# Attention scores in two PSUM banks in place of four, written one slot ahead by two ordered pairs of row groups

## The reference, cut to what matters

```python
# second (_L2_xattn_ref)
scores = jnp.einsum('bhqd,bhkd->bhqk', qh, kh) / jnp.sqrt(dh)
scores = jnp.where(merged == 1, NEG_INF, scores)
attn = jax.nn.softmax(scores, axis=-1)
out = jnp.einsum('bhqk,bhkd->bhqd', attn, vh)
# last (_L3_xattn_ref)
scores = jnp.einsum('bhqd,bhkd->bhqk', q, k) / jnp.sqrt(jnp.float32(dh))
scores = jnp.where(scores == 0, NEG_INF, scores)
attn = jax.nn.softmax(scores, axis=-1)
```

## Time and profile before

| | |
|---|---|
| median of 3 runs | 1098.03 us (1096.59 to 1098.26) |
| the profiled execution's own time | 1100.99 us |
| its span, first to last instruction | 1099.2 us |
| PE busy | 911.5 us, 83% |
| DVE busy | 556.6 us, 51% |
| ACT busy | 444.9 us, 40% |
| POOL busy | 392.7 us, 36% |
| mean granted clock of TensorE | 0.890 |

### The profile page before, as it was taken

The page is one execution under the profiler, slowest core; times in us unless marked ns, Lnnn a source line. Parts: engine busy times, 40 slices in busy tenths (PEclk is TensorE's granted clock), DMA queues, the critical chain, the costliest instruction groups (busy, mean ns, idle before and its releaser), DMA issues. The chain is left out here.

```text
span 1099.2 us, 18929 instructions
## 1 busy us (share of the span) xinstructions
PE 911.5 (83%) x5718; PEld 623.4 (57%) x5719; DVE 556.6 (51%) x1282; ACT 444.9 (40%) x874; POOL 392.7 (36%) x726
## 2 busy tenths in 40 slices
PE   6688887888699999935888889997999997888773
PEld 4466655776566666723555556653666674555441
DVE  4688865674722222227988735220211235767854
ACT  4355555552132222214555542221222225656634
POOL 5566642364400000036766512110000035766630
PEclk9799999996599999975878999998999996988965
DMA  5599510011211111127310030002111121110002
GB/s 182 156 365 385 183 48 1 20 49 39 101 57 58 61 58 61 53 75 275 136 32 18 2 130 30 23 30 72 38 48 48 39 43 23 16 16 11 2 1 77
DMA packets 74397, 84.17 MB, mean 77 GB/s; under 512 B 8299, under 2 KB 66643, under 8 KB 74323
## 3 DMA queue, kind: packets, MB, share of 16 engines
q1 hardware_dynamic: 68179, 70.65, 19.1%
q0 software_dynamic: 6144, 12.59, 4.2%
HBM read 45.73 MB, written 37.49 MB: 76 GB/s over the span
## 5 line engine op out<-in xcount | busy, mean ns | idle before, releaser
L1808 PE MATMUL PS<-WE,tmp 128*128 x496 | 186.9, 521 | 0.0
L1388 DVE TENSOR_TENSOR tmp<-PS,tmp 128x352 f32<-128x352 f32 (+1 forms) x78 | 47.4, 608 | 255.5 <-ACT tmp L918 255.5
L589 POOL TENSOR_TENSOR tmp<-tmp,small 128x616 f32<-128x616 f32 x96 | 116.7, 1216 | 92.7 <-DVE small L1053 92.5
L918 ACT ACTIVATE tmp<-PS 128x352 f32<-128x352 f32 (+1 forms) x78 | 41.4, 530 | 214.6 <-PE PS L1808 214.6
L1808 PEld LDWEIGHTS PS<-WE,tmp 128*128 128x128 f32 x496 | 91.8, 195 | 60.5 <-issue 36.1
L804 ACT ACTIVATE tmp<-PS 128x768 f32<-128x768 f32 x96 | 77.9, 811 | 104.9 <-PE PS L1584 104.2
L1830 PE MATMUL PS<-WE,tmp 128*128 (+1 forms) x418 | 101.0, 380 | 2.1 <-DVE tmp L1413 2.1
L1582 PE MATMUL PS<-ident,tmp 128*128 128x128 f32 x384 | 69.2, 309 | 34.6 <-POOL rsx L576 22.4
L1483 PE MATMUL PS<-ident,XN 128*128 128x128 f32 x208 | 40.4, 327 | 63.4 <-ACT XN L740 57.8
L740 ACT ACTIVATE XN<-X,SHIFTS,RSTDS 128x256 f32<-128x256 f32 x104 | 56.3, 590 | 71.9 <-POOL SHIFTS L531 71.8
L556 POOL DMA_INDIRECT WE<-ys,slot_u x16 | 15.8, 988 | 182.8 <-DMA ys<-tmp 179.7
(11 more groups left out here) (253 smaller groups left out, 1698.4 us busy)
## 6 DMA issues: line engine op xcount, KB each, us to landing
xs_regions<-WE SPq DMA_DIRECT2D x11, 1536.0 KB, 13.5
ys<-tmp SPq DMA_DIRECT2D x62, 128.0 KB, 1.7
WE<-in_L_w SPq DMA_DIRECT2D x16, 352.0 KB
tmp<-xs_regions SPq DMA_DIRECT2D x39, 128.0 KB, 2.0
WE<-in_L_rgT SPq DMA_DIRECT2D x8, 512.0 KB
WE<-in_L_ruT SPq DMA_DIRECT2D x8, 512.0 KB
WE<-in_L_rdT SPq DMA_DIRECT2D x8, 512.0 KB
tmp<-xs SPq DMA_DIRECT2D x23, 128.0 KB, 2.0
```

What stands on the lines that cost most here:

```text
L589: pool.tensor_tensor(sc, sc, spread(mx[:, q], SK), ALU.add).then_inc(shifted, 1)
L1808: last = pe.matmul(PS[:, 2 * q + k, 0:F], XS[:, q, c], w, start=c == 0, stop=c == G - 1)
```

## The change

`TWO_SCORES` switches `a2` and `a3` over; `a0` stays as it was. A unit's scores now lie in 2 banks of 308 columns, and units alternate between banks 0, 1 and banks 2, 3. Row groups 0 and 2 write the left half of the two banks (`half` 0), row groups 1 and 3 the right half (`half` 1), and a new semaphore, `half_psum`, keeps the second pair behind the first. In slot s PE writes the scores of unit s+1: the first pair where `scores(s)` stood, the second pair behind `values(s-3)`. The first pair waits for `s_taken` of unit s-1. ACT and DVE read the same 616 numbers as 2 by 308 in place of 4 by 154.

```diff
+        def s_psum_of(stage, k):
+            if TWO_SCORES[stage]:
+                return PS[:, 2 * (k % 2):2 * (k % 2) + 2, 0:2 * PAIR]
+            return PS[:, 0:CHUNKS, 0:PAIR]
...
+                def half_scores(k, half):
+                    b, g, t = k // UNITS, k % UNITS // T, k % T
+                    if half == 0:
+                        if stage != "a2":
+                            pe.wait_ge(q_ready, q0 + b + 1)
+                        else:
+                            pe.wait_ge(xt_ready, norms + order["in", b] + 1)
+                        after(pe, s_taken, u0 + k - 1 if k >= 2 else 0)
+                    else:
+                        pe.wait_ge(half_psum, HALVES[stage] + k + 1)
+                    for c in (half, half + 2):
...
+                        last = pe.matmul(PS[:, 2 * (k % 2) + c // 2, half * PAIR:(half + 1) * PAIR], q, KBD[at, g, b],
+                                         start=True, stop=True)
+                    last.then_inc(s_psum if half else half_psum, 1)
...
-                    if 0 <= s < NU:
+                    if TWO_SCORES[stage]:
+                        if s == 0:
+                            half_scores(0, 0)
+                            half_scores(0, 1)
+                        if 0 <= s < NU - 1:
+                            half_scores(s + 1, 0)
+                            if s < 3 + LATE[stage]:
+                                half_scores(s + 1, 1)
+                    elif 0 <= s < NU:
                         scores(s)
...
                         values(s - 3 - LATE[stage])
+                        if TWO_SCORES[stage] and s < NU - 1:
+                            half_scores(s + 1, 1)
```

More of the change, by code:

```diff
@@ L202, in build @@
         PT_PSUM = transposed[:, 0:PTW]
-        S_PSUM = PS[:, 0:CHUNKS, 0:PAIR]
+        TWO_SCORES = dict(a0=False, a2=True, a3=True)
+        HALVES = {stage: NU * sum(TWO_SCORES[early] for early in ("a0", "a2", "a3")[:i]) for i, stage in enumerate(("a0", "a2", "a3"))}
+        def s_psum_of(stage, k):
+            if TWO_SCORES[stage]:
+                return PS[:, 2 * (k % 2):2 * (k % 2) + 2, 0:2 * PAIR]
+            return PS[:, 0:CHUNKS, 0:PAIR]
         x_loaded = [sem(f"x_loaded{b}") for b in range(B)]; wk_loaded = sem("wk_loaded"); wv_loaded = sem("wv_loaded"); vecs_loaded = sem("vecs_loaded"); mask_ready = sem("mask_ready"); zeros_ready = sem("zeros_ready"); ctx_loaded = sem("ctx_loaded"); small_loaded = sem("small_loaded")
@@ L212, in build @@
         blocks_psum = sem("blocks_psum"); blocks_ready = sem("blocks_ready")
-        s_psum = sem("s_psum"); s_copied = sem("s_copied"); s_taken = sem("s_taken"); max_ready = sem("max_ready"); shifted = sem("shifted"); exp_done = sem("exp_done")
+        s_psum = sem("s_psum"); half_psum = sem("half_psum"); s_copied = sem("s_copied"); s_taken = sem("s_taken"); max_ready = sem("max_ready"); shifted = sem("shifted"); exp_done = sem("exp_done")
         veps_ready = sem("veps_ready"); rstd_ready = sem("rstd_ready")
@@ L769, in scores_scaled @@
                     after(act, s_taken, u0 + k - 1)
-                    act.activation(Z[:, k % 2].rearrange("p (c n) -> p c n", c=CHUNKS), S_PSUM, ACT.Copy,
+                    scores = s_psum_of(stage, k)
+                    act.activation(Z[:, k % 2].rearrange("p (c n) -> p c n", c=scores.shape[1]), scores, ACT.Copy,
                                    scale=1.0 / FAR).then_inc(s_copied, 1)
@@ L1042, in biased_scores @@
                     sc = SC[:, k % 4]
+                    scores = s_psum_of(stage, k)
+                    n = scores.shape[1]
                     if stage == "a3":
                         dve.wait_ge(s_copied, k + 1)
-                        dve.scalar_tensor_tensor(out=sc, in0=S_PSUM, scalar=0.0, in1=Z[:, k % 2], op0=ALU.is_equal,
+                        dve.scalar_tensor_tensor(out=sc, in0=scores, scalar=0.0, in1=Z[:, k % 2], op0=ALU.is_equal,
                                                  op1=ALU.subtract, reverse1=True).then_inc(s_taken, 1)
                     else:
-                        bias = BIAS[:, row].unsqueeze(1).unsqueeze(1).to_broadcast([P, CHUNKS, 2, SK])
-                        dve.tensor_tensor(sc.rearrange("p (c h k) -> p c h k", c=CHUNKS, k=SK),
-                                          S_PSUM.rearrange("p c (h k) -> p c h k", k=SK), bias, ALU.add).then_inc(s_taken, 1)
+                        bias = BIAS[:, row].unsqueeze(1).unsqueeze(1).to_broadcast([P, n, HG // n, SK])
+                        dve.tensor_tensor(sc.rearrange("p (c h k) -> p c h k", c=n, k=SK),
+                                          scores.rearrange("p c (h k) -> p c h k", k=SK), bias, ALU.add).then_inc(s_taken, 1)
                     dve.drain()
@@ L1574, in scores @@
                     last.then_inc(s_psum, 1)
+                def half_scores(k, half):
[9 more added lines that the diff above has]
+                    for c in (half, half + 2):
+                        at = slice(2 * DH * c, 2 * DH * (c + 1))
+                        q = XT[at, b, g, 1 + t * P:1 + (t + 1) * P] if stage == "a2" else QT[at, b % 2, g, t * P:(t + 1) * P]
+                        last = pe.matmul(PS[:, 2 * (k % 2) + c // 2, half * PAIR:(half + 1) * PAIR], q, KBD[at, g, b],
+                                         start=True, stop=True)
+                    last.then_inc(s_psum if half else half_psum, 1)
                 def transposes(k):
```

## The result

| | before | changed |
|---|---|---|
| median of 20 runs each | 1095.84 us (1090.35 to 1101.87) | 1113.21 us (1098.10 to 1122.46) |
| the profiled execution's own time | 1100.99 us | 1114.04 us |
| its span and mean granted clock | 1099.2 us, 0.890 | 1112.2 us, 0.888 |

On the 1098.03 us of the prediction that is 1110.9 us: outside the range of 1087 to 1107, and on the side of rival B, beyond its 1107.

What follows compares the result with a forecast made beforehand. It took `a2` and `a3` as close to several limits at once (PE, DVE), partly at halved TensorE clock. `a3` 5.5 - 8.3 = -2.8 and `a2` 3.7 - 4.7 = -1.0 took 1098.03 to 1094.2 us; range 1087 to 1107.

Steps and rivals of the forecast that it cites:

- rival B: Second pair on the path between values and projection or queries, clock as before: +9.2 us, 1107 us; chance 0.27.
- The clock in `a2`: Long half-clock stretch averted -2.5 us, three second pairs cheaper -1.2, short falls -1.0: -4.7 us in all.
- the long stretch of `a2` at half clock: 13 us in `a2` with PE busy 12.07; at full clock some 10.5 would do, -2.5 us.
- The clock in `a3`: Three of four falls between 950 and 1050 us averted, two at 2.9 us and one at 2.5: -8.3 us.
- The second pair on PE: Two of the four score products cost 0.45 us at full clock, 0.85 at half clock.
- Where it is on the path: Second pair ahead of queries or projections, plus stage starts, clock as before: `a3` +5.5 us; `a2` +3.7 after DVE's -2.4.
- the start of `a3`: Unit 0's two pairs back to back +0.8 us, unit 2's pairs ahead of batch 1's queries +0.8 again.
- Fewer waits of DVE: DVE's 7.3 us of waiting for scores in `a2` goes; a third is kept, -2.4 us.
- The 0.9 us in hand ahead of L980: In `a2` the out projection ends 0.9 us before DVE needs it; two second pairs use that up.
- The waits that stay: First pair still waits for `s_taken`, 2.1 us in 7 times in `a3`, and runs under ACT's copy of T at no cost.
- C: Clock held in `a3` only, as 0.45 us may not fill `a2`'s logits wait: +0.9 us, 1099 us; chance 0.18.
- the prediction's last sentence: Wrong above all if the clock falls in the same places, or PE's more even work brings new falls.

Runs made afterwards that it cites:

- e7: Kernel before, plus four unused full-array products behind the values in `a2`'s slots with logits; ratio 0.9962, median 1093.50 us.
- e8: e7 plus three unused full-array products ahead of T in every fourth slot of `a3`; ratio 0.9909 to the kernel before, median 1088.38 us.
- e13: e8 with its unused products over 32 rows of the array in place of 128; ratio 0.9997 to the kernel before, median 1097.49 us.
- e14: Kernel before with the change in `a2` alone, plus the unused products of e7 in `a2`; ratio 0.9979, median 1096.06 us.
- e4: Changed kernel with the second pair's products issued twice from unit 4 on; ratio 1.0154 to the kernel before, median 1115.18 us.
- e11: Kernel before with the change in `a3` alone, both pairs together ahead of the values; ratio 1.0049, median 1103.45 us.
- e2: Kernel before with the change in `a3` alone; ratio 1.0091, median 1104.97 us.
- e9: Changed kernel plus the unused full-array products of e8 in both stages; ratio 0.9993 to the kernel before, median 1098.97 us.
- e10: e3 plus the unused full-array products of e8 in both stages; ratio 0.9929 to the kernel before, median 1091.33 us.
- e3: Changed kernel with the second pair always right behind the first, ahead of the values; ratio 1.0079 to the kernel before, median 1104.81 us.

## Why the prediction was wrong

**The clock in `a2`: the step that failed.** The prediction booked the long stretch of `a2` at half clock as averted, with more: -4.7 us, so -1.0 for the stage. The stage took 12.8 us more in the trace, with 83 us at half clock where it had 58, and over the runs the kernel with `a2` alone has 22 us more. That an idle PE precedes the loss of the clock was right (e7, e8). That the second pair fills the stretch was not: behind the logits it leaves 0.91 us of 1.34, and the clock falls. Nor was it sound to take a 32-row product for as good as any other: the prediction itself says that no row shows it, and in e13 such products leave 0.26 us and the clock still falls. That the loss is the clock's is shown: with full products in the same stretches `a2` takes 143.5 us changed (e14) and 143.6 unchanged (e7). Why the stretches at half clock last 17 to 20 us stays open. The likely reading is that the added step keeps PE behind: it is busy 4.9 of 5 us in them, so it doesn't catch up, and small products are much of what it does. That is only argued, and against it as the whole cause speaks e4, with more 32-row work and 236 us at half clock.

**The clock in `a3`: right in kind.** Three falls were to be averted, and in the trace three are gone, by the place of the pair, as e11 shows. The price was a little high: a batch of four slots takes 19.9 us before, with a fall in it, and 17.72 in e8 without, so 2.2 us a fall where 2.9 and 2.5 were taken. Without the stretch from its first T to its fourth, the stage took 136 us before and takes 134 in the changed kernel. Over the runs of e2 nothing of the gain is seen (225 us at half clock, as beside it), and no trace of a typical run of e2 says where it went.

**The second pair on PE: right.** 0.45 and 0.85 us were taken; the chain has 0.46 and 0.81. Two row groups cost what four cost, 0.47 at full clock.

**Where it is on the path: right in place, the start of `a3` too small.** Rival B's +5.5 for `a3` and +3.7 for `a2`, 9.2 together, compare with 6 to 8 at held clock (e9 against e8, less the clock's 3). But the parts differ. In `a3` the times from T to T tell: a batch of four slots at full clock takes 17.72 us in e8, 17.82 in e10 and 18.18 in e9 and in the changed kernel. That is one pair of 0.46 a batch, as forecast, and nearly nothing when the pairs stand together. At the start of `a3` the prediction had +1.6; from the first T to the fourth it is 13.0 us before, 18.5 changed, 17.0 in e3 and e11, and with the fillers 14.2 (e8), 18.9 (e9) and 15.7 (e10). So 5 us or so go there, three times what was booked. Without fillers 4.0 of the 5.5 are there with the pairs together too, so they go with the scores written ahead and split; with fillers it is 1.5 of 4.7. In kernels whose `a3` is as before the same stretch varies from 12.3 to 14.2 us. These slots run at half clock from 939 on, so part may be the clock; the runs don't divide it. In `a2` the path was to cost 3.7 us: e14 stands some 2 above e7, and the intervals take in both 3.7 and nothing.

**Fewer waits of DVE: right that they go, wrong that a third is kept.** 7.3 us fell to 1.1, and nothing was kept; the traces of e7 and e14 show where all of it went. The 0.9 us in hand ahead of L980 were used up, which the prediction named.

**The waits that stay: right.** L780 is still what DVE waits for in `a3`. What the prediction left out is ACT's wait for the queries' product, which now stands behind the pair: 8.2 us became 15.9.

**The rivals.** B had the mechanism and about the size of the path; it held the clock unchanged, so that it came nearest is partly luck: in the trace the clock rose in `a3` and fell in `a2`. C named the right place, the wait behind the logits that 0.45 us may not fill, and had `a3`'s clock rise; the traces show that, and the runs of e2 don't (225 us at half clock, as beside it). It took `a2`'s clock as unchanged, where it got worse. The range ended at B and so had no room for "the clock gets worse", although the prediction's last sentence names it.

## What to carry to other kernels

Before counting on added work to hold TensorE's clock, test it with unused products of the very shape in the very place; here the shape made 0.9997 of 0.9909 for the same 1.15 us of PE. And compare what is put into an idle stretch with its length: 0.45 us in a stretch of 1.34 left 0.91, and the clock fell as before; in one of 1.41 it left 0.78, and the clock stayed. If idle stretches of PE precede falls of the clock, filling them with full-array products that nobody reads is worth a run of its own, before any reordering. Splitting a group of products that run side by side costs a whole step for each part: put the parts where PE waits anyway, and not ahead of a product that the next engine waits for.

## What the runs showed of the hardware

- At 1.2 GHz the clock can stay down for 17 to 20 us with PE busy 97 to 99%; from 550 to 565 and 615 to 625 us of the changed kernel it is busy 4.9 of each 5 us, at 0.50 in every row.
- In the changed kernel the clock fell behind 0.91 and 0.88 us of idling in `a2` (547.38 and 608.73 us), and not behind 0.68 there (592.00) or 0.78 in `a3` (990.97); in e13 it fell behind 0.26 us with 32-row products ahead of it.
- An fp32 product of 128 columns takes the same time over 32 rows as over 128 (1.15 and 1.16 us for eight instructions), yet in the same idle stretches the kernel was at half clock for 224 us with the former and 189 with the latter (e13, e8; 228 with neither).
- Two row groups of scores took 0.46 us, four took 0.47.
- Runs of one kernel spread with the mean granted clock: the changed kernel's go from 1098 to 1122 us, with 206 to 276 us at half clock.
